# Four step sums in flight in the plain passes of a graph-network kernel

## The reference, cut to what matters

```python
h = x @ W
msg = h[src] * norm[:, None]
out = jax.ops.segment_sum(msg, dst, num_segments=n_nodes)      # layer 0, twice
msg_sum = jax.ops.segment_sum(feature[src], dst, num_segments=n)  # layer 2
```

## Time and profile before

| | us |
|---|---|
| median of 3 runs | 6748.66 (6747.69 to 6758.79) |
| span of the profiled execution | 7795.8 |
| POOL busy in it | 4491.4 (58%) |
| PE busy | 4038.3 (52%) |
| DVE busy | 3241.9 (42%) |
| ACT busy | 1099.4 (14%) |

### The profile page before, as it was taken

How to read it: one execution, slowest core, us unless ns; L and a number is a source line. 1 busy time by engine, 2 the same in 40 slices (tenths; PEclk the granted TensorE clock), 3 DMA queues, 4 the chain that set the end, 5 groups by cost and what they waited for, 6 DMA issues and landing times.

```text
span 7795.8 us, 105357 instructions
## 1 busy us (share of the span) xinstructions
PE 4038.3 (52%) x24944; PEld 3239.4 (42%) x24945; DVE 3241.9 (42%) x8240; ACT 1099.4 (14%) x2520; POOL 4491.4 (58%) x4619
## 2 busy tenths in 40 slices
PE   0333334333333455555558868823333347777776
PEld 0323323333233345544557767713333334444443
DVE  4222213222124555555578888842221243333335
ACT  0000000000001222222233343310000021111112
POOL 4666665666664555555535535546666635555553
PEclk9656656556566676667789989955665565555555
DMA  3111112111111333333347757711111111111111
GB/s 98 44 45 45 45 46 54 44 46 45 45 45 29 118 118 119 118 118 119 120 151 224 225 176 228 223 47 44 45 45 45 45 41 38 38 39 38 39 38 39
DMA packets 354854, 637.41 MB, mean 82 GB/s; under 512 B 85485, under 2 KB 120442, under 8 KB 354170
## 3 DMA queue, kind: packets, MB, share of 16 engines
q0 software_dynamic: 127936, 263.97, 13.5%
q10 hardware_dynamic: 105408, 191.94, 7.9%
q1 hardware_dynamic: 121466, 181.04, 6.8%
HBM read 500.81 MB, written 135.79 MB: 82 GB/s over the span
## 4 chain that ended last, share of the span: by engine, by line
another core or an unknown queue 35%; PE 24%; issue 16%; DVE 12%; DVEq 5%; DMA 4%; ACT 3%; ACTq 1%; SPq 0%; POOL 0%; POOLq 0%
PE ps_sum L606 15%; PE ps_u L661 4%; PE ps_u L639 4%; DMA hots<-hot_rows 3%; DVE zu L1190 2%; DVE onehot L1000 2%; DVEq L241 2%; DVE acc L1014 1%; DVEq L1014 1%; DVE logit L1199 1%; ACT hots L808 1%; PE ps_a L656 1%; DVE prob_n L1174 1%; ACT onehot L818 1%
## 5 line engine op out<-in xcount | busy, mean ns | idle before, releaser
L525 POOL DMA_INDIRECT ring<-table,rows_idx x3920 | 3874.4, 988 | 2436.8 <-issue 1126.9
L606 PE MATMUL ps_sum<-ring,onehot 128*128 x5856 | 1202.3, 380 | 2328.5 <-DVE onehot L1000 1047.7
L606 PEld LDWEIGHTS ps_sum<-ring,onehot 128*128 128x128 f32 x5856 | 1078.6, 280 | 2452.1 <-issue 2450.5
L1014 DVE TENSOR_TENSOR acc<-ps_sum,acc 128x128 f32 x1708 | 492.2, 288 | 3140.0 <-remote 2336.3
L606 PE MATMUL ps_sum<-msg,onehot 128*128 128x128 f32 x7808 | 1479.8, 349 | 33.3 <-POOL msg L311 21.9
L606 PEld LDWEIGHTS ps_sum<-msg,onehot 128*128 128x128 f32 x7808 | 1285.1, 249 | 432.0 <-issue 396.5
L639 PE MATMUL ps_u<-u_parts,hots 128*128 x8784 | 763.8, 239 | 790.1 <-ACT hots L808 364.8
L1000 DVE SCALAR_TENSOR_TENSOR onehot<-dst,minus_row,iota 128x512 f32<-128x512 f32 x1220 | 913.8, 749 | 239.8 <-issue 211.9
L639 PEld LDWEIGHTS ps_u<-u_parts,hots 128*128 128x128 bf16 x8784 | 619.9, 106 | 915.0 <-issue 880.4
L311 POOL TENSOR_TENSOR msg<-ring,prob_n 128x512 f32<-128x512 f32 x488 | 516.9, 1059 | 614.6 <-DVE prob_n L1174 581.8
L1190 DVE TENSOR_TENSOR zu<-ps_u,ring 128x512 f32<-128x512 f32 x732 | 503.1, 687 | 594.8 <-remote 283.8
(11 more groups left out here) (149 smaller groups left out, 1919.9 us busy)
## 6 DMA issues: line engine op xcount, KB each, us to landing
hots<-hot_rows ACTq DMA_DIRECT2D x488, 256.0 KB, 3.5
ring<-z_rows SPq DMA_DIRECT2D x392, 256.0 KB, 3.6
ring<-table,rows_idx POOLq DMA_INDIRECT x3920
hot_rows<-hots ACTq DMA_DIRECT2D x244, 256.0 KB
z_rows<-ring SPq DMA_DIRECT2D x196, 256.0 KB
table<-acc SPq DMA_DIRECT2D x9, 1024.0 KB, 5.1
x<-in_x SPq DMA_DIRECT2D x1, 3328.0 KB, 11.6
table<-h SPq DMA_DIRECT2D x4, 832.0 KB, 4.4
```

What stands on the lines that cost most here:

```text
L525: nc.gpsimd.indirect_dma_start(out=ring[:, j, t * P:(t + 1) * P], out_offset=None, in_=tables[p], in_offset=bass.IndirectOffsetOnAxis(ap=r ...
L606: last = nc.tensor.matmul(ps_sum[k % 2][:, 0:P], lhsT=onehot[:, k % HOTS, t, :], rhs=rows(t), start=(t == 0), stop=(t == TILES - 1))
L1014: V.tensor_tensor(acc_flat[:, at], ps_sum[k % 2][:, 0:P], acc_flat[:, at], ALU.add)\
```

## The change

In the plain passes a step sum goes to one of four banks (`ps_sum[0]`, `ps_sum[1]`, `ps_u[0]`, `ps_u[1]`), so PE waits for the add of four steps back, not two. DVE makes the one-hot of step s ahead of the add of step s-3, not s-1; three adds trail at the end of a pass. `key_row` and `chunk_tab`, the two tables that the engines load numbers from, become 16-bit unsigned integers instead of 32-bit ones, in all passes. The number of slots in the ring, the one-hot buffers, and the other passes' order stay.

```diff
-        key_row = sb("key_row", [1, CHUNKS], i32)
+        key_row = sb("key_row", [1, CHUNKS], u16)
...
-        chunk_tab = sb("chunk_tab", [1, 256], i32)
+        chunk_tab = sb("chunk_tab", [1, 256], u16)
...
+        plain_sums = (ps_sum[0], ps_sum[1], ps_u[0], ps_u[1])
+        assert UNROLL % len(plain_sums) == 0 and HOTS >= len(plain_sums)
...
-            def sum_step(s, k, p, rows):
+            def sum_step(s, k, p, rows, sums=ps_sum):
 
                 pe.wait_ge(hot_ready, s + (1 + STEPS * p))
-                if not (s.fixed and s + STEPS * p < 2):
-                    pe.wait_ge(step_added, s + (STEPS * p - 1))
+                if not (s.fixed and s + STEPS * p < len(sums)):
+                    pe.wait_ge(step_added, s + (STEPS * p + 1 - len(sums)))
                 for t in range(TILES):
-                    last = nc.tensor.matmul(ps_sum[k % 2][:, 0:P], lhsT=onehot[:, k % HOTS, t, :],
+                    last = nc.tensor.matmul(sums[k % len(sums)][:, 0:P], lhsT=onehot[:, k % HOTS, t, :],
                                             rhs=rows(t), start=(t == 0), stop=(t == TILES - 1))
                 last.then_inc(step_summed, 1)
...
-                    sum_step(s, k, p, lambda t: rows[:, t * P:(t + 1) * P])
+                    sum_step(s, k, p, lambda t: rows[:, t * P:(t + 1) * P], plain_sums)
...
-            def add_step(s, k, chunk, p):
+            def add_step(s, k, chunk, p, sums=ps_sum):
...
-                V.tensor_tensor(acc_flat[:, at], ps_sum[k % 2][:, 0:P], acc_flat[:, at], ALU.add)\
+                V.tensor_tensor(acc_flat[:, at], sums[k % len(sums)][:, 0:P], acc_flat[:, at], ALU.add)\
                  .then_inc(step_added, 1)
 
             def plain_pass(p):
+                ahead = len(plain_sums) - 1
+
                 def body(s, k, chunk, have):
                     if have(0):
                         hot(s, k, chunk(0), p)
-                    if have(1):
-                        add_step(s.back(1), k - 1, chunk(1), p)
-                over_steps(dve, ENGINE.DVE, body, 1)
+                    if have(ahead):
+                        add_step(s.back(ahead), k - ahead, chunk(ahead), p, plain_sums)
+                over_steps(dve, ENGINE.DVE, body, ahead)
                 dve.wait_ge(step_added, STEPS * (p + 1))
```

More of the change, by code:

```diff
@@ L46, in build @@
           w_edge, b_edge, w_out, b_out, gamma, beta, out):
-    fp32, bf16, i32 = mybir.dt.float32, mybir.dt.bfloat16, mybir.dt.int32
+    fp32, bf16, i32, u16 = mybir.dt.float32, mybir.dt.bfloat16, mybir.dt.int32, mybir.dt.uint16
     ALU = mybir.AluOpType
```

## The result

The changed kernel took 6943.9 us (median of 4 runs, 6928.3 to 6953.65), the kernel before 6749.41 us on the same chip (4 runs, 6747.69 to 6758.79): a ratio of 1.0286, 95% interval 1.0270 to 1.0302. It is 195 us slower. Forecast were 6745 us and no change, with 6790 us as the range's upper end.

A forecast was written before the change was run, and what follows sets the result against it. POOL's issue of gathers was taken to bound the plain passes, so nothing is won there: 6748.66 + 0 - 3 (starts and ends) = about 6745 us, with an 8-in-10 range of 6635 to 6790.

The forecast's parts named there:

- the fifth, "The tables of two bytes": Two-byte loads, open on DVE and PE in CAPS1, EDGE, CAPS2, CAPS3: taken as 0, bounds -58 and +117 us.
- rival C: Two-byte loads cost more on DVE and PE in CAPS1 and EDGE: 58 us at 1.5 times; chance 0.10.
- The floor of the plain passes: CONV1, CONV2, MEAN: POOL's issue of 784 gathers, 1.25 us apart, sets 980 us a pass, 4.02 us a step.
- parts (1) to (4): Plain passes: PE's later-step wait, DVE's reordering, SP's slot freeing and the extra banks, with nothing won in a steady-POOL run.
- The gap between span and median: Span 7795.8 us, median 1047 us less: likelier POOL's slot waits belong to the profiled execution, at most 86 us in runs.
- Rival B: Plain passes: POOL's slot waits are as large in runs; 107 to 429 us saved, half gives 6534 us; chance 0.17.
- A: Plain passes: runs hold 86 us of POOL waits, deeper pipeline takes 52 us, giving 6697 us; chance 0.17.
- D: Plain passes: one-hots beside POOL slow its gathers, + 30 us (177 us at the end), giving 6779 us; chance 0.06.

The follow-up runs named there:

- e13: Changed kernel with a four-byte chunk table for CAPS2 and CAPS3 alone, on an on-time chip: 6774.06 us, 1.0026 against the kernel before.
- e9: Kernel before with '& 255' masks in its waits, four-byte tables, on an on-time chip: 6746.63 us, 0.9997 against the kernel before.
- e10: Pipelining alone: changed kernel with four-byte tables and masks, on an on-time chip: 6753.52 us, 1.0009 against the kernel before.
- e1: Kernel before with '& 255' masks in its waits, four-byte tables, on a late chip: 7805.31 us, 1.0042 against the kernel before.
- e2: Pipelining alone: changed kernel with four-byte tables and masks, on a late chip: 7775.09 us, 1.0002 against the kernel before.
- e5: Changed kernel with a four-byte chunk table for CAPS2 and CAPS3 alone, on a late chip: 7799.72 us, 0.9940 against the kernel before.
- e6: Kernel before with masks, late chip; tripled loads meant for CAPS2 and CAPS3 weren't in the program: 7868.05 us, 1.0027 against the kernel before.
- e12: e9 with eight extra unread products on PE behind each plain-pass sum, on an on-time chip: 6770.92 us, 1.0038.
- e15: e12 again, meant for a late chip but run on an on-time one: 6777.93 us, 1.0030.
- e14: e9 with LONG 24 instead of 12, so CAPS2 and CAPS3 load 28 numbers 10 times, not 16 numbers 20 times: 6747.68 us, 0.9988.

## Why the prediction was wrong

**The step that failed is the fifth, "The tables of two bytes".** I took 0 "as the nearest row is the same instruction with the same count of numbers", and set twice the price as the upper end. Measured is 3.1 times for 8 numbers on DVE, 3.3 times for 16. The number of rounds and the passes named were right: 40 rounds of CAPS2 and CAPS3, 122 elsewhere. So was the sign of rival C, but not its place or its chance. I put it "at the head of each round of four steps on DVE and PE in CAPS1 and EDGE"; there, and in the plain passes, the dearer loads and the pipelining together cost some 20 us (e13), the most in CAPS1 and none in EDGE, as POOL's gathers set the time. They lie open where no gather gives cover, at the longer rounds of CAPS2 and CAPS3, and cost 170 us there, 4.2 us a round for 2.5 to 2.7 us more of loading; PE's products at the lower clock after a stop add 1.5 us a round, which is about the rest. The places that I listed would, at the measured price, have given about 250 us, 150 of them in CAPS1 and EDGE and 100 in CAPS2 and CAPS3, so the right price alone would have given a loss of that order, but most of it in the wrong passes. A look at the earlier trace rows would have said so: 443 of 510 us on PE in CAPS2 is a pass without slack, and a load stands at the head of its every round.

The floor for a load that I cited from the Trainium skill (DMA: Bandwidth & Descriptors, Latency and other measured facts) is about 600 ns. It holds for 8 four-byte numbers here (592 and 598 ns), but 4 numbers took 337 ns and 8 two-byte ones 1828, so it bounds neither side. The 337 ns stood in the earlier trace rows already, and a floor says nothing of what a wider or narrower number costs above it; I should not have concluded from it that the width is free.

**The floor of the plain passes held.** On time they take 991 to 993 us, with or without pipelining (e9, e10), near the 980 us of 784 gathers at 1.25 us. The parts (1) to (4) together: +0.1% between e9 and e10 against 0 forecast, within what can be told.

**The gap between span and median was read half right.** That POOL's waits were for the most part not in the timed runs holds, though 168.5 us of the 1133.2 were, twice the 86 us that I allowed. But I gave them to the profile, and that is wrong: in late groups every run has them, profiled or not (e1, 7795.54 to 7809.9 us), and on time the profiled execution lacks them too (e9's is 6743.28 us). So the trace and the median must have come from two chips, or from one in two conditions; which, the record doesn't say. A gap of 1047 us between a span and a tight median should have made me ask.

**Rival B** has its answer on the late chips: a quarter of 429 us, 107 us, was the least I gave it (8 us in 36 is 0.22 and not a quarter, so 95 us by its own figures); measured are 30 us between e2 and e1, 9 to 16 us a pass, and 13 to 19 us a pass between e5 and e6. PE's wait for one-hots fell by four fifths, and POOL's for slots in CONV1 only from 139.5 to 113.5 us. That is what I had put against B, that the slot still waits for the sum; no run tests it by itself. **A** is nothing (e10). **D** is nothing: 980 ns for the mean gather after, 976 in e9.

## What to carry to other kernels

A change of type in a table that engines load registers from is a change of time on every engine that reads it: count its loads in all stages, not in those that the change is about, and look first at the stage without slack. Where a trace's span and the median of the runs differ by far more than the runs do among themselves, compare the trace with nothing before it is known that both are of the same kind of chip. Depth behind a wait helps only up to the signal that the bottleneck itself waits for.

## What the runs showed of the hardware

- Loading numbers to registers: four bytes each take 0.35, 0.60 and 1.10 us for 4, 8 and 16 numbers on DVE (0.063 us a number), two bytes each (unsigned; no other two-byte type ran) 0.95, 1.83 and 3.60 us (0.22). What in a two-byte load takes the time isn't shown. SP's loads of 14 numbers take 2.86 to 2.87 us with either width; why its four-byte loads are slow too is open.
- On chips 14 and 15, and in the trace, sums of the gathering passes are announced late, while in CAPS2 and CAPS3, where POOL issues no gathers, they aren't. In CONV1 of that trace the add starts 3 us behind the modelled end of its sum in the median, more than 17 us in one step of ten and 31 us at the most; in e9 it is 0.7 us at the most. CAPS2 and CAPS3 take the same time on either kind of chip (507 and 509 us there, 508 and 511 in e9), and the five gathering passes are 146, 145, 374, 148 and 204 us longer: the kernel takes 1030 to 1100 us more. Whether the sum or only the message is late, and why, is open: e12 and e15 were to tell whether PE's idleness matters, and met no such chip.
- After a stop of 3.41 us PE ran two steps at the lower of its two levels (12 products in 1.54 us instead of 0.83), while in e9, with loads of 1.1 us, and in e14, with loads of 1.88 us, the granted clock of the pass stays at 0.99 to 1.00.
